# Two more row tiles fetched by SyncE: 30 and 18 rows behind its loads in place of 28 and 16

## The reference

```python
h = jnp.maximum(_layernorm(x, axis=-1), 0.0)
...
msg = jax.nn.relu(h[src] + edge_attr)
agg = jax.ops.segment_sum(msg, dst, num_segments=h.shape[0])
z = h + agg
z = jax.nn.relu(z @ W1 + b1)
x = x + z @ W2 + b2
```

## Time and profile before

| | |
|---|---|
| median of 3 runs | 1404.91 us |
| lowest to highest | 1401.84 to 1407.89 us |
| profiled execution, its own time | 1406.43 us |
| its span | 1404.6 us |
| TensorE clock granted, mean | 0.991 of full speed |
| row tiles / GpSimd's gathers in the loop | 20 / 1091 |
| TensorE's candidate tiles | 488 |

### The profile page before, as it was taken

One profiled execution on the slowest core, in us unless ns is written; L12 is line 12 of the kernel. 1 busy time (PEld: TensorE's weight loads), 2 busy tenths in 40 slices (PEclk: granted clock), 3 DMA queues, 4 the chain that ended last, 5 costly groups with the idle time before them and its releaser, 6 DMA issues.

```text
span 1404.6 us, 26588 instructions
## 1 busy us (share of the span) xinstructions
PE 1369.4 (97%) x7788; PEld 708.6 (50%) x7788; DVE 1216.5 (87%) x1869; ACT 1063.3 (76%) x1165; POOL 1057.5 (75%) x1114
## 2 busy tenths in 40 slices
PE   7897999999999999999999999999999999999997
PEld 4443555555555555555555555555555555555554
DVE  8698988888888888888888888888888989878887
ACT  6775877787777877777777777887787777877772
POOL 7777777777777777777777777777777777777775
PEclk8999999999999999999999999999999999999999
DMA  7223233233232332333323233233232323323231
GB/s 247 65 58 83 73 91 86 70 95 85 69 90 66 94 85 69 90 74 86 85 68 95 68 88 85 69 95 86 70 85 69 95 68 88 85 69 94 62 86 29
DMA packets 70785, 116.54 MB, mean 83 GB/s; under 512 B 34522, under 2 KB 35950, under 8 KB 70638
## 3 DMA queue, kind: packets, MB, share of 16 engines
q1 hardware_dynamic: 34302, 76.39, 17.3%
q0 software_dynamic: 35328, 36.25, 13.1%
q10 hardware_dynamic: 1008, 2.19, 0.4%
HBM read 111.39 MB, written 3.34 MB: 82 GB/s over the span
## 4 chain that ended last, share of the span: by engine, by line
PE 82%; DVE 6%; POOL 5%; ACT 2%; issue 2%; DMA 1%; DVEq 0%; SPq 0%; POOLq 0%; ACTq 0%
PE ps_cand L1305 80%; POOL gath L397 5%; PE ps L426 1%; DVE parts L1027 1%; ACT keyhot L738 1%; DVE gath L979 1%; DVE picked L972 1%; DMA gath<-h_table,idx_all 1%; ACT keyhot L745 1%; DMA src_k<-src_keys 1%; PE ps L460 1%; DVE ends L1037 1%; DVE ps_edge L1020 1%; DVE table_lo L899 0%; PE ps L450 0%
## 5 line engine op out<-in xcount | busy, mean ns | idle before, releaser
L397 POOL DMA_INDIRECT gath<-h_table,idx_all x1091 | 1040.9, 954 | 334.4 <-issue 316.5
L1305 PE MATMUL ps_cand<-table_hi,keyhot 128*128 128x448 f16 x3388 | 1197.3, 353 | 18.0 <-DVE picked L972 13.7
L1305 PE MATMUL ps_cand<-table_lo,keyhot 128*128 128x448 f16 x3388 | 1196.2, 353 | 0.0
L738 ACT ACTIVATE keyhot<-key_pair,key_bias 128x512 f16<-128x512 f16 (+1 forms) x854 | 532.6, 705 | 115.1 <-PE ps_cand L1305 113.9
L1305 PEld LDWEIGHTS ps_cand<-table_hi,keyhot 128*128 128x128 f16 x3388 | 331.8, 98 | 333.0 <-DVE picked L972 9.7
L1305 PEld LDWEIGHTS ps_cand<-table_lo,keyhot 128*128 128x128 f16 x3388 | 332.0, 98 | 301.3 <-issue 2.0
L745 ACT ACTIVATE keyhot<-keyhot,hot_bias 128x3584 f16<-128x3584 f16 (+1 forms) x122 | 397.4, 3258 | 3.9
L972 DVE TENSOR_TENSOR picked<-ps_cand,cand_mask 128x448 f32<-128x448 f32 x488 | 301.3, 617 | 81.8 <-PE ps_cand L1305 81.4
L979 DVE TENSOR_REDUCE gath<-picked 128x64 f32<-128x448 f32 x488 | 298.6, 612 | 4.2
L1027 DVE SCALAR_TENSOR_TENSOR parts<-ps_edge,side 128x832 f32<-128x832 f32 x242 | 235.3, 1014 | 0.0
L1037 DVE TENSOR_REDUCE ends<-parts 128x128 f32<-128x1664 f32 x122 | 228.7, 1875 | 0.0
(11 more groups left out here) (112 smaller groups left out, 189.2 us busy)
## 6 DMA issues: line engine op xcount, KB each, us to landing
edge_pair<-edges_t SPq DMA_DIRECT2D x62, 832.0 KB
gath<-h_table SPq DMA_DIRECT2D x2560, 0.2 KB
gath<-h_table,idx_all POOLq DMA_INDIRECT x1091, 2.4
key_pair<-key_table SPq DMA_DIRECT2D x61, 256.0 KB
h_table<-h_a SPq DMA_DIRECT2D x7, 224.0 KB, 2.7
part_x<-x_t SPq DMA_DIRECT2D x29, 48.0 KB
out<-part_out SPq DMA_DIRECT2D x29, 48.0 KB
x_c<-x_cols ACTq DMA_DIRECT2D x4, 256.0 KB, 4.7
```

Of the source, the lines that this page charges most:

```text
L397: nc.gpsimd.indirect_dma_start(out=rows[:, r, :], out_offset=None, in_=h_table, in_offset=bass.IndirectOffsetOnAxis(ap=idx[:, r:r + 1], ax ...
L738: last = nc.scalar.activation(keyhot[u % 2][:, a, 0:n], key[u][:, P * PE_MAX - n:], ACT.Abs, bias=key_bias[:, a:a + 1])
L1305: last = nc.tensor.matmul(bank[:, 0:D * CAND], keyhot[u % 2][:, a, i * P:(i + 1) * P], half[:, a, :, :].rearrange("p d b -> p (d b)"), sta ...
```

## The change

Two numbers change, and with them what the code works out from them.

```diff
-ROWS_AT = (28, 16)
+ROWS_AT = (30, 18)
 ROWS_A_LOAD = 16
 ROW_TILES = (TURNS - 1) * PAIRS * sum(ROWS_AT) // P
```

## The result

The changed kernel takes 1520.33 us, median of 5 runs (1519.37 to 1521.94), against 1404.91 before (also 5 runs by then, 1401.84 to 1407.89): a ratio of 1.0821 (95% interval 1.0805 to 1.0838), 115 us more. I had forecast 1402.5.

A forecast was written before the change was run, and what follows sets the result against it. TensorE and GpSimd were taken as level, GpSimd late from about 1060 us. 2.50 us saved less 0.15 gave about 2.4: 1406.43 becomes 1404.0, and 1402.5 us with the median 1.5 lower; range 1399.0 to 1407.5.

The forecast's parts named there:

- What bounds the kernel now: Whole kernel: TensorE and GpSimd level, TensorE setting the pace first, GpSimd the late one from about 1060 us.
- the tail: End of the kernel: the last big sum waits for GpSimd's last gathers, so the tail gets the full 2.50 us.
- GpSimd's term: GpSimd's queue: 1089 gathers for 1091, each 1.252 us, so everything behind them comes 2.50 us earlier.
- rival 1: Kernel's end: TensorE's last tiles hold the tail, only 0 to 1.4 us less, 1403.5 to 1404.9; chance 0.25.
- SyncE's term: SyncE's queue: four more rows and more register loads add 2.14 us per half turn, leaving 0.22 us; nothing charged.
- Rival 2: SyncE's queue from key load to key load becomes the bound: at 2.9 us added, 17 us slower, 1422; chance 0.06.
- the cover: Key loads on SyncE: some 15 us of lateness stay hidden before their use.
- TensorE's term: TensorE: four late waits go, a light chunk at slot 2 may add 0.6 us; last tile 0 to 1.4 us earlier.
- The DMA engines: DMA engines: 256 more packets in SyncE's queue, engines busy 0.31 of the time; nothing charged.
- Rival 3: DMA engines limit the gathers: the moved rows come back as later landings, no gain, 1404.9; chance 0.06.
- rule on issuers: Row loads moved to SyncE: all issuers share 16 DMA engines, moving saves only sequencer time; read strictly, 1404.9.

The follow-up runs named there:

- (28, 20): The changed kernel with 28 rows behind the keys and 20 behind the edges instead of 30 and 18, all loads aligned: 1403.5 us, ratio 0.9989 to the kernel before.
- the exchanged loads: The changed kernel with its two register loads behind the edges exchanged, first 2 numbers, then 16: 1403.61 us, ratio 0.9995 to the kernel before.
- (32, 16): The changed kernel with 32 rows behind the keys and 16 behind the edges instead of 30 and 18: 1403.1 us, ratio 0.9986 to the kernel before.
- (26, 18): The kernel before with 26 rows behind the keys and 18 behind the edges instead of 28 and 16: 1441.17 us, ratio 1.0262.
- (32, 20): The changed kernel with 32 and 20 rows, up to 32 numbers a load, 24 row tiles, 1087 gathers: 1416.68 us, ratio 1.0086 to the kernel before.

## Why the prediction was wrong

**What bounds the kernel now: right.** Two level engines and SyncE with 2.4 us of room. (28, 20) and the exchanged loads, at 1403.5 and 1403.6, stand on the edge that this reading drew. What I added for the tail, that it hangs on GpSimd's gathers, did not hold with two gathers fewer, as the next term shows.

**GpSimd's term, 2.50 us less: right in what it counted, but the tail passed to TensorE.** It can be read in the (32, 16) kernel, which has the gathers of the change without its slow load. It is faster by 0.14%, 2.0 us (0.7 to 3.4), where I had 2.4. Its last gather ends at 1393.2 us where it was 1397.3, 4.1 earlier. But before, the chain that ended last left TensorE at 1382.36 us for GpSimd's last gathers, and now it stays with TensorE (start, duration, what):

```profile
1379.94 10.70 PE ps_cand L1305 x56
1390.64 0.26 PE ps L426 x4
```

In the (28, 20) kernel the chain has no gather behind 1340 us either. That is rival 1. The measured gain can't tell the two apart, since its interval holds both my 2.4 and the 0.75 that TensorE saved (below); that it came out near 2.4 doesn't speak for my reason. VectorE's wait for gathers is no measure of the gain: in 1060 to 1380 us it fell from 26.4 us to 12.1 in the one kernel and to 24.6 in the other, whose profiled execution was the shorter of the two (spans of 1402.0 and 1400.0 us). First (32, 16), then (28, 20):

```profile
DVE ps_edge L1020 <- DMA gath<-h_table,idx_all: 12.1, 12, 2.7
...
PEld ps_cand L1305 <- ACT keyhot L745: 0.6, 1, 0.6
...
DVE ps_edge L1020 <- DMA gath<-h_table,idx_all: 24.6, 19, 2.1
...
PEld ps_cand L1305 <- ACT keyhot L745: 0.7, 1, 0.7
```

**SyncE's term: this is the step that failed.** I wrote "a load adds 1.05 us to a row's step", took 48 more loads at that price, 0.84 us per half turn, and bounded it from above "With the longest load (1.302, plus about 0.1 of moves)". The number of loads was right, the price per row too. The price of a load was not one price. All 187 loads of before read 4, 8, 12 or 16 numbers from a multiple of 4, because 28, 16, 44 and 128 are all multiples of 4; the largest of them bounds only its own kind. 30 brought a start at 2 and a size of 14, of which no row of before said anything. Of the 51 slow loads each took 3.54 - 1.18 = 2.36 us more, 120 us in all, and 59 loads of 14 took 1.46 where those of 12 took 1.02, 26 us. The order of the changed kernel showed the batches of 14 and 2; I counted them and did not ask where they start. Put together from the two traces, the register loads take 388.6 us where they took 201.9: 3.1 us more per half turn, where I had 0.84. With the 1.30 for the rows and the moves the addition is some 4.5 us, against a room of 2.36. The shortage of 2.1 us that this estimate leaves is near the 2.3 measured (24.2 less 21.8, below).

**Rival 2 was the case, its mechanism as described.** The place (from key load to key load), the way (keys late, ScalarE waits, TensorE waits) and the price (the shortage times the half turns, less a cover) hold. Its condition, an addition over 2.61 us, came from the price of one form of load, not from a row step that grows, which is what I had named for it. From the first keys that ScalarE waited for, used at 245.5 us, to those of chunk (30,0) at 1454.5 the 50 half turns take 24.2 us each (the short eighth ones included). Before, the same keys are used at 245.5 and 1337.6, 21.8 us each: that difference, 117 us, covers the whole result. Up to 245.5 us nothing was lost; that was the cover. The key load at which the waits began was issued at 242.0 where it had been at 225.1, so the cover was 17 us where I took "some 15". (I took the landing from a load of 224 KB as the nearest in size; the page also has loads of 256 KB, at 4.7 us, which my doubled 2.7 covers. The keys at 676.95 landed in 3.4.) With such a cover the sums of prices for (26, 18) and (32, 20) said 1450 and 1405 to 1422 us, and 1441 and 1417 were measured. I gave it 0.06, because I took what is known of a queue's pieces to be a bound on new pieces.

**TensorE's term: it holds, in both traces of aligned loads.** The four late waits are gone, and the two that are left, one of 0.6 us in 300 to 1000 us and the one shown above, are those that I had charged to the light chunks at slot 2: TensorE's chunks (11,3) and (24,3) begin as soon as their hots end. The second of them in the (32, 16) kernel:

```profile
1112.55 3.29 ACT keyhot L745
1115.84 0.05 issue
1115.88 9.25 PE ps_cand L1305 x48
```

From the same chunk's start (275.94 us before, 277.05 and 274.84 in the two kernels) to the end of its last candidates (1390.29, 1390.64 and 1388.44) TensorE needs 1114.35 us before and 1113.59 and 1113.60 now: 0.75 us less, in the middle of the 0 to 1.4 that I had. That these chunks start 1.1 us later in one trace and 1.1 earlier in the other is as large as the effect, and no run says why.

**The clock.** The lower granted clock of the changed kernel (0.96 in 600 to 644 us against 1.00) goes with TensorE's waits and makes its matmuls a mean of 359 ns for 353; it is a consequence: in 300 to 600 us all lines of the chain but the unnamed "issue" are SyncE's.

**The DMA engines.** Their share is 0.30 in the same stretch, and a gather's mean is unchanged. Rival 3 finds nothing for it, and the Trainium skill's rule on issuers that I weighed (page "DMA: Bandwidth & Descriptors", section "Issuing engines are not separate DMA queues") spoke of the right resource: the issuer's time is all that is moved, and here it was the dearer issuer's.

Two statements of the Trainium skill bear on the load. The page "DMA: Bandwidth & Descriptors", section "Latency and other measured facts", gives a register load a floor of about 600 ns and says that the compiler unrolls it by four to spread that. The page "Runtime: NRT & Kernel Launch", section "Instruction fetch mechanics", says of loads of registers from HBM that they take about 200 ns a register even in bulk. Here the smallest loads take 0.47 to 0.56 us, less than that floor, and the measurement decides. The 200 ns is what a register costs in these loads from SBUF when the start is not at a 16-byte boundary (0.20 us), but from such a boundary four registers cost 0.21 together. Neither page speaks of the start. A fetch of 16 bytes at once would fit these prices; no run looked into it, and it is not shown.

## What to carry to other kernels

Before a price from a trace is put on new instructions of the same kind, list the sizes and starts that the old ones had: a maximum over loads that are all aligned is no bound for one that is not. Register loads of i32 numbers on SyncE want starts at multiples of 4 numbers (16 bytes) and sizes that are multiples of 4; where a count does not allow it, read the odd piece first (2 and then 16 instead of 16 and then 2 gave back 117 us here). And when an engine with 2 us of room per period gets 2 us more work, price each new piece by itself, since the rest of the kernel turns on it.

## What the runs showed of the hardware that I had not expected

- A register load of 16 four-byte numbers on SyncE takes 1.19 us from a 16-byte boundary and 3.5 us from 4, 8 or 12 bytes past one; 32 and 64 byte boundaries make no difference (1.18 us at 16, 32 and 48 bytes past a multiple of 64).
- 14 numbers from a 16-byte boundary (1.38 to 1.46 us) cost more than 16 (1.19).
- 8 bytes in the place of a table's numbers in SBUF, with no instruction added, removed or moved, are the whole difference between 1409 and 1618 us (the two kernels with the moved table).
